# A planner's rank for the last three entries: by remaining work in place of entry number, and one more draw of jitter

## The reference, cut to what matters

```
x = ln(x + L0_attn(x))        # linear attention (elu+1) of 16x16 heads per token, then a GELU MLP 256->1024->256
x = ln(x + L0_xattn(x, ctx))  # attention on ctx, 16 heads, local window of 64
x = ln(x + L0_ffn(x))         # 6 cells, each an 8-head softmax attention between earlier nodes
x = ln(x + L1_attn(x))        # causal linear attention with RMS-normed heads
x = ln(x + L1_xattn(x, ctx))  # attention on ctx with a mask, 16 heads
x = ln(x + L1_ffn(x))         # a linear map by FFTs, folded into one 256x256 matrix
```

## Time and profile before

| | us |
|---|---|
| median of 3 runs | 3439.23 |
| the profiled execution, its own time | 3441.86 |
| its span, first to last instruction | 3440.1 |
| TensorE (PE) busy | 3101.7 (90%) |
| VectorE (DVE) busy | 2330.8 (68%) |
| ScalarE (ACT) busy | 1701.0 (49%) |
| GpSimd (POOL) busy | 1182.5 (34%) |
| mean granted TensorE clock | 0.967 of full speed |

### The profile page before, as it was taken

How to read it: one execution, slowest core, us unless ns; L and a number is a source line. 1 busy time by engine, 2 the same in 40 slices (tenths; PEclk the granted TensorE clock), 3 DMA queues, 4 the chain that set the end, 5 groups by cost and what they waited for, 6 DMA issues and landing times.

```text
span 3440.1 us, 75934 instructions
## 1 busy us (share of the span) xinstructions
PE 3101.7 (90%) x29836; PEld 2294.8 (67%) x29836; DVE 2330.8 (68%) x5044; ACT 1701.0 (49%) x3496; POOL 1182.5 (34%) x1308
## 2 busy tenths in 40 slices
PE   7889889999999999989999999999999999989876
PEld 6766666676666666666666766666676666666654
DVE  6586667768686866768677686867767686465543
ACT  1245454555546455554545555464554545454442
POOL 7876007062341615234170623416052341100000
PEclk8899999999999999999999999999999999999996
DMA  7211001010101101011110101011010110100000
GB/s 223 72 56 35 20 29 35 26 47 20 43 27 38 29 26 47 20 39 32 35 32 25 49 20 43 27 38 29 22 52 20 39 32 20 32 14 10 10 10 4
DMA packets 123275, 122.77 MB, mean 36 GB/s; under 512 B 9776, under 2 KB 122672, under 8 KB 122800
## 3 DMA queue, kind: packets, MB, share of 16 engines
q1 hardware_dynamic: 122928, 117.91, 11.6%
HBM read 113.69 MB, written 4.19 MB: 34 GB/s over the span
## 4 chain that ended last, share of the span: by engine, by line
PE 63%; DVE 15%; ACT 7%; POOL 7%; issue 7%; DMA 1%; SPq 0%; DVEq 0%; POOLq 0%; ACTq 0%
PE banks L748 18%; PE banks L740 16%; PE banks L886 7%; DVE nmx L1260 6%; PE banks L947 5%; PE banks L908 5%; ACT work L1491 4%; POOL work L1641 3%; PE banks L733 2%; POOL work L1651 2%; PE banks L954 2%; PE banks L851 2%; POOL work L1661 1%; DVE added L1278 1%; ACT work L1393 1%
## 5 line engine op out<-in xcount | busy, mean ns | idle before, releaser
L748 PE MATMUL banks<-work,weights 128*128 128x256 f32 x3584 | 848.6, 385 | 22.5 <-DVE work L1284 10.4
L748 PEld LDWEIGHTS banks<-work,weights 128*128 128x128 f32 x3584 | 662.5, 190 | 153.6 <-issue 43.4
L1260 DVE TENSOR_REDUCE nmx<-banks 128x4 f32<-128x1024 f32 (+1 forms) x567 | 609.5, 1115 | 200.5 <-PE banks L886 199.0
L1491 ACT ACTIVATE work<-banks 128x1024 f32<-128x1024 f32 (+3 forms) x703 | 598.4, 908 | 270.5 <-PE banks L920 251.4
L740 PE MATMUL banks<-weights,work 128*128 128x256 f32 x2688 | 665.8, 395 | 20.2 <-DVE work L1288 7.6
L740 PEld LDWEIGHTS banks<-weights,work 128*128 128x128 f32 x2688 | 506.6, 195 | 131.9 <-issue 37.0
L1651 POOL TENSOR_TENSOR work<-work 128x512 f32<-128x512 f32 x256 | 417.6, 1655 | 85.1 <-DVE work L1221 81.9
L908 PE MATMUL banks<-work 32*128 32x256 f32 (+1 forms) x5120 | 367.1, 397 | 70.1 <-DVE nmx L1260 42.1
L886 PE MATMUL banks<-work 32*128 32x256 f32 (+1 forms) x5120 | 361.2, 398 | 70.5 <-DVE nmx L1260 29.7
L1641 POOL TENSOR_TENSOR work<-work 128x512 f32<-128x512 f32 x256 | 335.5, 1333 | 132.0 <-DVE work L1217 108.6
L1695 POOL TENSOR_TENSOR work<-work,row 128x512 f32<-128x512 f32 x64 | 93.0, 1463 | 836.8 <-PE banks L733 836.8
(11 more groups left out here) (160 smaller groups left out, 3540.7 us busy)
## 6 DMA issues: line engine op xcount, KB each, us to landing
weights<-in_w_all SPq DMA_DIRECT2D x322, 256.0 KB, 2.7
work<-in_w_setup SPq DMA_DIRECT2D x41, 256.0 KB, 5.0
work<-in_ctx SPq DMA_DIRECT2D x32, 256.0 KB, 3.0
work<-in_x SPq DMA_DIRECT2D x16, 256.0 KB, 3.0
out<-work SPq DMA_DIRECT2D x16, 256.0 KB, 2.2
weights<-in_w_all SPq DMA_DIRECT2D x1, 3072.0 KB, 15.6
row<-in_rows SPq DMA_DIRECT2D x1, 1280.0 KB, 9.0
mrow<-in_mask SPq DMA_DIRECT2D x16, 32.0 KB, 3.3
```

The source lines that it names most:

```text
L748: ins = e.matmul(b[:, m * 256:m * 256 + 256], wslot(w)[:, k, m * P:m * P + P], xin[:, k, :], start=(k == 0 and (m == 0 or closed)) if star ...
L1260: ins = e.tensor_reduce(nmax(s, n)[:, 2 * p + j:2 * p + end, :], b.rearrange("p j (c n) -> p j c n", c=NC)[:, :, :, 0:w], AX, ALU.max, neg ...
L1491: ins = e.activation(dst, b.rearrange("p j (c n) -> p j c n", c=NC)[:, :, :, 0:w], ACT.Exp)
```

## The change

Two edits, both in the planner. The number compared first is cut off at `NB - 3` = 13, so the steps of entries 13, 14 and 15 have the same rank, and among them the tail decides, behind the 0.5 for a change of mode. And `SEEDS` has one more number, so all tails, of all entries and of the setup, are multiplied once more by factors of up to 1.08.

```
-SEEDS = (519167, ..., 91813, 237616)
+SEEDS = (519167, ..., 91813, 237616, 902168)
...
             for i, t, n in sorted(waiting[e], key=lambda w: (
-                    ((2.5 if e == "SP" else 1.5) if w[0] < 0 else w[0]) + (0 if kept_mode(w[2]) else 0.5), w[1], w[2])):
+                    ((2.5 if e == "SP" else 1.5) if w[0] < 0 else min(w[0], NB - 3)) + (0 if kept_mode(w[2]) else 0.5), w[1], w[2])):
```

More of the change, by code:

```diff
@@ L71 @@
 RSLOT = {n: i for i, n in enumerate(ROWS)}
-SEEDS = (519167, 634534, 875864, 704644, 851259, 37516, 529412, 612800, 351972, 744357, 284174, 279811, 642892, 207843, 86077, 805968, 561942, 32633, 126238, 798516, 91813, 237616)
+SEEDS = (519167, 634534, 875864, 704644, 851259, 37516, 529412, 612800, 351972, 744357, 284174, 279811, 642892, 207843, 86077, 805968, 561942, 32633, 126238, 798516, 91813, 237616, 902168)
 SLOTS = 10
```

## The result

The kernel after has a median of 3426.18 us over 19 runs. Beside it the kernel before has 3450.19 us over 19 runs. The ratio is 0.994, with a 95% interval of 0.9924 to 0.9955: 0.6% faster, some 21 us, where 52 were forecast and nothing above 3420 was in the range. One of the 19 executions of the kernel before was a slow one, 4288.86 us; it is left out of the ratio and of the 21 us, and the median of the other 18 is 3447.28.

A forecast was written before the change was run, and what follows sets the result against it. TensorE's work was taken as the bound, idle mainly while entry 15 ends alone; 3441.9 - 52 (end) + 0 (redraw) = 3389.9, less 2.6 for the profiled execution standing above the median, gave 3387 us, range 3354 to 3420.

The forecast's parts named there:

- The split that I chose: After entry 12's store: 229.8 us of work at rate 0.897, 177.5 at 0.848, plus drain: 475.5 us, gain 52.
- The drain: Last 20 us of the kernel: 10 us unfilled, between 2 if all three entries drain at once and 14 if one alone.
- Edit 1 ahead of entry 12's store: From 2299.58 us on: same PE work in another order, hidden by three other entries in flight, cost nothing.
- My sign: Entry 12's store moving over 17 us either way, with periods as far apart as before, would refute the redraw's zero.
- The rule that I weighed: At the end: interleaving regimes helps, the common rank does the reverse; by it alone the sum is the lower end, 494.3 us.
- Edit 2, the redraw at 0: One more factor on tails, all entries and setup: redraws near ties, adds no work, taken as 0 us.
- my ends of -34 and +50: Redraw's bounds over 12 periods, all at 198.1 or all at 205.1 us; about a third of each allowed in the range.
- Rival (c): Middle: redraw lengthens each period through waits for head maxima; decisive from 5.8 us per period, 3466 at 207.5; chance 0.04.
- The bunching by mode at 0: Entries 13 to 15: the 0.5 bunches steps of one tiling mode, gains 3 us at most, delays long tails; taken as 0.
- (a): Whole end: head steps block one another over PSUM banks, rate 0.848 with late drain, gain 33, so 3406 us; chance 0.18.
- (b): End: no levelling, entry 15 still ends alone some 120 us after its `again` load, 3439 us; chance 0.08.
- The streamed weights: SP's queue: lockstep entries each load the same weight; four uses, 7.8 us, outlast a 2.7 us load; cost nothing.

The follow-up runs named there:

- late_rank: Kernel before with the common rank of entries 13 to 15 starting only when the planner has finished entry 12, old 22 seeds: 0.9857, 3401.52 us; again 0.9852, 3391.08 us.
- rank_only: Kernel before with edit 1 alone, the common rank from the start, old 22 seeds: ratio 1.0006, 3454.81 us against 3452.71.
- pe_only: Kernel before with the common rank only in PE's queue, from the start; DVE, ACT and POOL keep entry numbers; 22 seeds: 0.9946, 3453.33 us.
- past_mix: Kernel before with the common rank only for steps past the first linear attention (from z2_t on), 22 seeds: 0.9953, 3434.52 us.
- past_x0: Kernel before with the common rank only for steps from the first head on, 22 seeds: 0.9892, 3435.42 us; repeated 0.9928, 3416.97 us.
- other_seed: Kernel before, old rank, with an arbitrary 23rd seed (2): ratio 1.0255, 3535.89 us.
- seed_only: Kernel before with edit 2 alone, the 23rd seed with the old rank: ratio 1.0045, 3463.77 us.
- after_again: The changed kernel unaltered, measured once more against the kernel before: ratio 0.993, 3429.43 us.
- no_mode: Changed kernel without the 0.5 for a change of tiling mode among entries 13 to 15, against the kernel before: 0.9882, 3429.75 us; again 0.9938, 3428.65 us.
- late_best: Kernel before with the common rank from entry 12's end and a 23rd seed picked by the planner's end time: 0.98, 3397.55 us; again 0.9877, 3395.94 us.

## Why the prediction was wrong

**The end: right, in part by luck.** The forecast for the stretch after entry 12's store was 475.5 us. late_rank, which does this and only this, takes 477.6, and its gain is 51 us where the sum had 52. The split that I chose (0.897, then 0.848, then a drain) works out to 0.857 on average; measured were 0.842 in late_rank and 0.865 in the changed kernel. The terms are less exact than their sum: in the first 256.2 us late_rank has a rate of 0.870 and 7 us less work done than the 229.8 of the sum, and this is hidden by a total of 402 us of work where I had 407.3. The rest, 0.818, is near my 177.5 us in 219.3, 0.809. The drain was 8 us against my 10: the last 20 us of late_rank hold 10.79 x 0.94 = 10.1 us of full-clock work, which take 12 us at 0.848. The last pieces of the three interleave. This is the timeline of PE in the kernel after, at its very end:

```profile
3412.12 5.42 PE L740 MATMUL banks<-weights,work 128*128 128x256 f32 x24 [0.19 <-DVE work L1288]
3417.49 0.66 PE L733 MATMUL banks<-ident,work 128*128 128x128 f32 x4
3418.92 1.97 PE L740 MATMUL banks<-weights,work 128*128 128x256 f32 x8 [0.78 <-ACT work L1418]
3420.72 0.63 PE L733 MATMUL banks<-ident,work 128*128 128x128 f32 x4
3422.14 1.97 PE L740 MATMUL banks<-weights,work 128*128 128x256 f32 x8 [0.78 <-ACT work L1418]
3423.94 0.60 PE L733 MATMUL banks<-ident,work 128*128 128x128 f32 x4
3425.23 1.99 PE L740 MATMUL banks<-weights,work 128*128 128x256 f32 x8 [0.69 <-ACT work L1418]
```

Three `y_o` products in one piece, then `f_t` and `f` of the three in turn with gaps of 0.7 to 0.8 us. The one chain of the kernel before has gaps of up to 3.2 us here, and at a lower clock each piece takes longer, 3.75 us for a product that takes 1.97 above:

```profile
3428.72 1.12 PE L733 MATMUL banks<-ident,work 128*128 128x128 f32 x4 [3.18 <-DVE work L1201]
3430.61 3.75 PE L740 MATMUL banks<-weights,work 128*128 128x256 f32 x8 [0.78 <-ACT work L1418]
```

**Edit 1 ahead of entry 12's store: this step failed.** The prediction costed it at nothing, "the same work in another order", hidden by three other entries in flight. rank_only against late_rank shows what it costs: 1.0006 against 0.9857, the whole gain. In the changed kernel, 0.994 against 0.9857, it is some 29 us, which is the distance between the 52 us forecast and the 21 measured. My sign pointed at the wrong edit: a store of entry 12 that moves by more than 17 us was to speak against the redraw's zero. It moved by 74 us, and 50 of them are made in the periods in which the common rank acts. (It acts from entry 14's first steps on, not from entry 13's, since 13 by itself has nobody to be level with.)

Why it costs is shown only down to the entries' order. The cover that the prediction counted on is other entries with work to fill TensorE while the oldest is in its LayerNorms and last heads. In my reading these entries must be in different stages: levelled, they are in heads or in the linear attention at the same time and have less full-array work to offer. Shown are the lost time in entry 12's period (a rate of 0.772 at a clock of 0.90, and steps of the first heads and of the linear attention side by side in its worst 80 us), that PE's order alone brings it (pe_only), and that the plan has the longer periods already. How it divides between heads, `band` steps and mix steps is only bounded, by past_mix and past_x0.

The rule that I weighed, that interleaving regimes helps (the Trainium skill, Perfetto Trace Analysis, Optimization Strategy), was put beside the wrong stretch. By it the end should have suffered, and there the trace doesn't agree: late_rank's end takes 477.6 us, where the sum by that rule had 494.3. (Over all levelled kernels the lost time in the end is 20 to 46 us.) In entry 12's period the trace agrees in part: in the 80 us shown, POOL is busy for 52.85 us against 36.92 in late_rank, while TensorE's full-clock work is 49 against 74. But DVE is no busier than in late_rank, 61.69 against 65.34.

**Edit 2, the redraw at 0: its size hangs on the rank beside it.** Alone it costs 0.45%, 15 us, within my allowance of a third of each end (-11 to +17). With the common rank from the start it gains 0.7%, some 23 us, beyond it (1.0006 to 0.994 or 0.993): the lost time goes from 90 to 65 us, 14 of it in entry 11's period and 13 in the end. With the late rank nothing shows (0.9857 to 0.985). That the changed kernel is faster than before at all is owed to the redraw, which I had at 0; that it gained and did not cost was no part of my reasoning.

The frame was wrong too. The periods of 198.1 and 205.1 us don't belong to the order: rank_only, whose plan is that of the kernel before up to entry 14's first steps, has 200.7 and 199.3 us for the same two. And what an arbitrary seed moved was not the steady period but the start: up to entry 4's store by 84 us against the profiled execution of before, by 62 and 68 against those of late_rank and rank_only, which have the 22 seeds too. That is outside both my ends of -34 and +50. Rival (c) looked for it in the period, where neither other_seed nor seed_only (200.5 us on average) has it.

The 24 us by which entry 9's store was late are mostly the spread between executions. rank_only, whose planned order is that of the kernel before up to there, has its entry 9 store at 2323.2 us, late_rank at 2324.8 and, on its second occasion, at 2306.3; seed_only has 2316.5. The profiled execution of the kernel before, 2299.6, was an early one: 3441.9 us, where its medians in the comparisons are 3440 to 3469. My sum was made against it, which puts the forecast's 3387 some 11 us low, but not its gain of 52.

**The bunching by mode at 0: right.** after_again and no_mode_again differ by 0.1%.

**Rivals.** (a), the head steps blocking one another, was placed at the end and has the loss of the right kind in the wrong place: its 33 us gain is near the measured 21, but the end's rate, 0.865 in the changed kernel and 0.842 in late_rank where (a) had 407.3 us in 494.3, 0.824, shows that this isn't how it came. (b), no levelling, is excluded by the three stores in 4.93 us. The streamed weights, which I held for covered, weren't tested by themselves; PE's waits on them in entry 12's period are one of 1.3 us, so they aren't the cause.

## What to carry to other kernels

A queue of independent jobs that is run oldest first leaves one job alone at its end; giving the last ones a common rank is worth what the lone stretch loses (here 51 us of 3450). But start it when the last job ahead of them is done: levelling earlier gave back all of it, in my reading because the younger jobs' difference in stage is what fills the bound engine until then. Where a planner simulates the order, ask its own end time first: here it had rank_only at 0.9994 and late_rank at 0.9865. It is no substitute for a run in small things: the 11 us of late_best were not on the chip. When an order comes from tuned random draws, take the draws and the rule together; the parts don't add up.

## What the runs showed that was not expected

One program's time moves by about 1% between executions, with its granted clock: the 29 runs of the kernel before beside the first four experiments go from 3430.93 us at a clock of 0.971 to 3468.91 at 0.962. Its median in a comparison went from 3440 to 3469 us. A ratio to the kernel before therefore carries some 0.5% that its interval doesn't show: the same kernel gave 0.9882 and 0.9938 (no_mode), and 0.98 and 0.9877 (late_best), with medians equal within 2 us. past_x0 gave 0.9892 and 0.9928, and there its own median moved by 18 us as well. Differences of this size between two variants are to be taken on one chip, one beside the other.

The granted clock is lower where TensorE is less full, in the middle as at the end: 1.00 over entry 12's period in late_rank with 184 of 198 us busy, 0.90 in the kernel after with 203 of 236, and 0.79 in the 80 us where it was busy for 62.
